# Offset convolution of a deformable convolution: 16 tiles of 32x32 reading x in place, instead of two 96x64 tiles reading shifted copies

## The chip, the cores and the metric

The kernel runs on one core of a Trainium2 chip. The metric is the device time of one execution in microseconds, median of several runs. A core has TensorE (PE, with its weight loads shown as PEld), VectorE (DVE), ScalarE (ACT), GpSimd (POOL) and SyncE (SP). Each takes its instructions in order, and they wait for one another through semaphores. Transfers are started from the queues of SP and ACT and carried out by 16 DMA engines.

## The reference

The input x has the shape (8, 16, 64, 64): batch, channels, rows, columns, in float32. Two layers follow each other. The first is layer norm, a depthwise 3x3 convolution, a channel gate, and attention in shifted 8x8 windows, which ends in a new x of the same shape. The second is a deformable convolution with batch norm, and the change is in its first step:

```python
om = conv_general_dilated(x, w_off, (1, 1), padding=[(1, 1), (1, 1)]) + b_off   # w_off: (27, 16, 3, 3)
off_y, off_x, mask = om[:, :9], om[:, 9:18], sigmoid(om[:, 18:])
py = off_y + row + ky - 1
px = off_x + column + kx - 1
# sampled = bilinear sample of x at (py, px) for each of the 9 taps, times mask
out = einsum('bckhw,ock->bohw', sampled, w) + b
return relu(batch_norm(out)) + x
```

So the offset convolution makes 27 channels for each of the 8 images: 9 vertical offsets, 9 horizontal offsets and 9 masks, from 16 input channels and 9 taps.

## The kernel before, in words

x lies on the 128 partitions as batch x channel (image b on partitions 16b to 16b+15), padded by one row and one column on each side, in the tile `xp` (66 rows of 66). PSUM is one tile `PS` of 8 banks of 512 float32 per partition.

The stages, in order: load of the constants and of x; layer norm; q, k and v; attention in a loop; a gate and the output projection, whose last step writes x into `xp` in 8 chunks of 8 rows (DVE, line 711, semaphore `xl_ready`); the **offset stage**, which this change is about; then the **sampling stage** (32 x 4 steps, lines 1297 to 1329), which takes most of the time; batch norm and the store of the result.

The offset stage goes over 8 chunks of 8 rows (512 columns of 64x8 positions). All engines follow an order that is written out by hand:

- SP copies `xp` four times three times into `xs` (line 336, 48 transfers): for each group g of two images and each kx, the 32 partitions of the group go to partitions 32kx to 32kx+31, shifted by kx columns. So the three horizontal taps stand under one another on 96 partitions. The copies go in four pieces of 16 rows, as soon as `xl_ready` says that the rows are there, and each piece has a semaphore `xs_in[j]`.
- PE, `offsets(n, u)` (line 1236): for each of two halves h, three matmuls (ky) for each of two sides accumulate 54 channels (2 images x 27) for 512 positions from 96 partitions.
- DVE (line 732) adds the bias and the column number to each of the two halves and writes them to `two[:, u]` (semaphore `om_out`). From the third chunk on it waits until the stores of the chunk two before have landed (`px_stored`).
- SP (h = 0) and ACT (h = 1) store the horizontal coordinates, 9 partitions at a time, into the scratch `px_scratch` in DRAM (`store_px`, line 315): four transfers each per chunk. ACT does this in between its evictions.
- PE, `first(n)` (line 1253): image rows for the first sampling (16 matmuls of 64x64 tiles, 144 columns, in three rounds), evicted by ACT at line 1053; and `to_samples(n, u)` (line 1260): 16 matmuls with 108 columns which transpose offsets and masks so that positions lie on partitions, evicted by ACT at lines 1061 and 1062.

PE's order is: offsets(0), offsets(1), first(0), to_samples(0), offsets(2), first(1), to_samples(1), and so on to offsets(7), first(6), to_samples(6), to_samples(7). After the last store has landed, SP loads the first coordinates back, spread over 64 partitions (`load_px`, line 345), and ACT makes the first weights of the sampling stage from them (lines 972 and 975).

At the start, SP issues x (2 of 8 chunks), the constants `cst` and the rest of x, and DVE's line 530 waits for the constants. PE's first matmuls wait for line 530. The weights of the offset convolution are laid out by DVE at lines 527 and 552.

```python
            def offsets(n, u):
                pe.wait_ge(om_out, free(n, 2))
                for h in range(2):
                    for ky in range(3):
                        for side in range(2):
                            ins = mm(PS[W * side:W * (side + 1), 2 * h + u, :], woff[0:96, ky, :],
```

Of the kernel before, what the change touches and what calls it, by code (L numbers as in the profile page):

```python
# [7 lines left out]
F32 = mybir.dt.float32  # L8
# [35 lines left out]
XS = (H + 2) * (W + 2)  # L44
# [8 lines left out]
_CCOLS = [("ident", P), ("eps_ln", 1), ("eps_bn", 1), ("bmask", B), ("bmod", PAIRS), ("h0", B), ("h1", B), ("ec", C), ("wide", 2 * P - B), ("spread", 4 * P), ("bmt", P), ("osum", P),  # L53
          ("negx", 1), ("kxadd", 1), ("xg", CH), ("pick", PAIRS * OC), ("jrel", NR),
          ("jabs", NBLK * NR), ("yabs", H * KK)]
# [15 lines left out]
def constants():  # L71
# [12 lines left out]
    put("h1", bm * (p[:, None] % C >= CS))  # L84
    put("ec", (p[:, None] % C == np.arange(C)).astype(np.float32))
# [6 lines left out]
    place = np.concatenate([[W * (g // 2) + OC * (g % 2) + k for k in range(OC)] for g in range(PAIRS)])  # L92
# [4 lines left out]
    put("xg", isx[:, None] * (np.arange(CH) % W)[None].astype(np.float32))  # L97
# [3 lines left out]
    y, k = np.meshgrid(np.arange(H), np.arange(KK), indexing="ij")  # L101
    put("yabs", (y - y % 2 + k // 3 - 1.0).reshape(1, -1) + (p // W)[:, None])
# [5 lines left out]
def build(nc, x, wpack, rpack, boff, consts, selc, out):  # L108
    ctx = ExitStack()
    with ctx:  # L110
# [6 lines left out]
        px_dram = nc.dram_tensor("px_scratch", (B, H, KK, W), F32, kind="Internal").ap()  # L117
# [7 lines left out]
        xp = sb("xp", [P, (H + 2) * (W + 2)])  # L125
        bd = sb("bd", [P, 6, P])
        MEAN, WQ, WK, WV, PO, SA = range(6)
        woff = sb("woff", [P, 3, W])
# [31 lines left out]

        xs_late = cut(PAIRS // 2 * XS)
        cut(None)
# [21 lines left out]
        xs_soon = cut2(PAIRS // 2 * XS)  # L184
        cut2(None)
# [4 lines left out]
        def xs_of(g):  # L190
            return (xs_soon, xs_late)[g // 2][:, g % 2 * XS:(g % 2 + 1) * XS]

# [67 lines left out]
        xs_in = [sem("xs_in%d" % j) for j in range(4)]  # L260
# [25 lines left out]
        def branches(eng, streams, passes):  # L286
# [6 lines left out]
            with eng.Else():  # L293
                with eng.Fori(0, PAIRS) as g:
                    with eng.Fori(0, NBLK) as band:
                        passes(g * NBLK + band, g, band)
                eng.nop()
# [25 lines left out]
        def _(sp):  # L323
# [26 lines left out]
            for u in range(2):  # L350
                sp.wait_ge(px_stored[u], 16 * B * NCH // 2)
            for line in range(0, PXR, GR):
                load_px(0, line, line)
# [1039 lines left out]
```

## Time and profile before

| | us |
|---|---|
| median of 3 runs | 880.37 (879.98 to 880.49) |
| the profiled execution, its own time | 876.57 |
| its span in the trace | 874.7 |
| busy: PE, DVE, ACT, POOL | 702.8, 723.9, 585.1, 598.7 |
| offset stage, first convolution matmul to the end of to_samples(6) | 257.09 to 325.84 |

The span is the time from the first to the last instruction in the trace. The time of an execution has a little around it (876.57 against 874.7). Engines work side by side, so their busy times don't add up to the span. What counts is who waits for whom, stage by stage.

### The profile page before, as it was taken

The numbers are of one execution on the slowest core, as the hardware profiler recorded it, in microseconds if no ns is written. First come the engines' busy times: TensorE is split into PE (matmuls) and PEld (weight loads), VectorE is DVE, ScalarE is ACT, GpSimd is POOL, SyncE is SP. The second block draws the span as 40 slices with busy tenths as digits, with TensorE's granted clock in tenths as the row PEclk, the third lists the DMA queues.
The fourth block names the chain that finished last, engine by engine and source line by source line (L and its number), as shares of the span: only waits on it lengthen the run. The fifth ranks groups of instructions, "written<-read, shape, count | busy, mean of one in ns | idle before, by whom it ended". The sixth has DMA issues, their size and how long they took to land.

```text
span 874.7 us, 30507 instructions
## 1 busy us (share of the span) xinstructions
PE 702.8 (80%) x12218; PEld 514.0 (59%) x12218; DVE 723.9 (83%) x975; ACT 585.1 (67%) x1088; POOL 598.7 (68%) x384
## 2 busy tenths in 40 slices
PE   4886888888699997888888787888888888777753
PEld 2532555656335666666667666776676666555542
DVE  1447999999532215999999999999999999999975
ACT  1445676776312327988878888879788888777615
POOL 2004887886140003989989999998899998999960
PEclk9787999999799997999999999999999999999987
DMA  4000000000076019555655555656555556555402
GB/s 165 0 1 0 1 1 0 0 0 0 0 179 150 15 22 216 158 151 141 157 164 138 152 151 143 160 138 164 156 141 146 161 143 165 159 150 152 111 3 97
DMA packets 29504, 90.77 MB, mean 104 GB/s; under 512 B 10446, under 2 KB 10574, under 8 KB 29134
## 3 DMA queue, kind: packets, MB, share of 16 engines
q1 hardware_dynamic: 26384, 88.25, 38.0%
q8 instruction: 91, 1.49, 0.8%
q10 hardware_dynamic: 3006, 0.84, 0.4%
q14 instruction: 23, 0.19, 0.1%
HBM read 79.11 MB, written 3.28 MB: 94 GB/s over the span
## 4 chain that ended last, share of the span: by engine, by line
DVE 45%; PE 33%; issue 15%; ACT 2%; DMA 2%; DVEq 1%; POOL 1%; ACTq 0%; SPq 0%; POOLq 0%
PE PS L1097 32%; DVE region L748 23%; DVE region L760 11%; DVE region L633 2%; DVE region L589 2%; DVE region L593 1%; DVE region L608 1%; DMA cst<-in_consts 1%; DVE region L595 1%; DVE region L578 1%; DVE region L590 1%; PE PS L1167 1%; DMA region<-px_scratch 1%; DVE region L575 0%; DVE region L535 0%
## 5 line engine op out<-in xcount | busy, mean ns | idle before, releaser
L1097 PE MATMUL PS<-region 64*64 64x144 f32 (+3 forms) x10112 | 459.4, 293 | 107.1 <-issue 75.7
L1097 PEld LDWEIGHTS PS<-region 64*64 64x64 f32 (+1 forms) x10112 | 343.8, 134 | 215.4 <-issue 185.5
L748 DVE TENSOR_TENSOR region<-PS,region 128x864 f32<-128x864 f32 x384 | 383.8, 1064 | 9.8 <-PE PS L1097 9.6
L488 POOL TENSOR_TENSOR region<-region 128x768 f32<-128x768 f32 x128 | 202.5, 1582 | 64.8 <-DVE region L748 64.8
L492 POOL TENSOR_TENSOR region<-region 128x864 f32<-128x864 f32 x128 | 224.1, 1751 | 18.6 <-POOL region L488 0.4
L975 ACT ACTIVATE region<-region 128x1152 f32<-128x1152 f32 x128 | 149.1, 1165 | 33.4 <-PE PS L1097 29.5
L972 ACT ACTIVATE region<-region,cst 128x1152 f32<-128x1152 f32 x128 | 159.3, 1244 | 5.7 <-DMA region<-px_scratch 4.4
L760 DVE TENSOR_REDUCE region<-region 128x32 f32<-128x960 f32 x128 | 148.3, 1159 | 1.5 <-POOL region L492 1.5
L411 POOL TENSOR_TENSOR region<-region,cst 128x1024 f32<-128x1024 f32 x32 | 61.1, 1911 | 50.5 <-ACT region L867 25.5
L1097 PE MATMUL PS<-wg,xp 64*64 64x144 f32 x1024 | 82.7, 289 | 5.4 <-issue 5.4
L1006 ACT ACTIVATE region<-x,cst (+2 forms) x288 | 86.7, 413 | 0.0
L1097 PEld LDWEIGHTS PS<-wg,xp 64*64 64x64 f32 x1024 | 67.1, 136 | 13.3 <-issue 12.2
L633 DVE SCALAR_TENSOR_TENSOR region<-region,wr (+4 forms) x57 | 73.7, 1293 | 0.1
L469 POOL TENSOR_TENSOR region<-region 128x648 f32<-128x648 f32 x32 | 41.8, 1306 | 41.5 <-ACT region L1014 41.5
L981 ACT ACTIVATE region<-PS 128x432 f32 (+3 forms) x75 | 35.9, 479 | 50.6 <-PE PS L1097 50.5
L416 POOL TENSOR_TENSOR region<-region,cst 128x512 f32<-128x512 f32 x32 | 43.9, 1373 | 1.7 <-DVE region L578 1.7
L1097 PE MATMUL PS<-region,woff 96*64 96x512 f32 x192 | 42.8, 592 | 0.8 <-DVE xp L711 0.8
L1053 ACT ACTIVATE region<-PS 128x432 f32<-128x432 f32 (+1 forms) x21 | 10.3, 490 | 45.3 <-PE PS L1097 44.8
L732 DVE SCALAR_TENSOR_TENSOR two<-PS,bcol,cst 128x512 f32<-128x512 f32 x16 | 11.3, 747 | 35.3 <-PE PS L1097 29.3
L887 ACT ACTIVATE region<-PS 128x512 f32<-128x512 f32 x32 | 19.1, 597 | 26.6 <-PE PS L1167 26.6
L882 ACT ACTIVATE region<-region 128x640 f32<-128x640 f32 x32 | 23.5, 735 | 12.4 <-DVE region L595 12.4
L1097 PEld LDWEIGHTS PS<-region,woff 96*64 96x64 f32 x192 | 16.6, 136 | 22.1 <-issue 20.5
(117 smaller groups left out, 609.9 us busy)
## 6 DMA issues: line engine op xcount, KB each, us to landing
region<-px_scratch SPq DMA_DIRECT2D x256, 288.0 KB, 4.3
out<-region SPq DMA_DIRECT2D x4, 512.0 KB, 3.0
x<-in_x SPq DMA_DIRECT2D x1, 1536.0 KB, 11.7
cst<-in_consts SPq DMA_DIRECT2D x1, 1234.5 KB, 8.6
region<-xp SPq DMA_DIRECT2D x8, 140.2 KB, 3.0
region<-xp SPq DMA_DIRECT2D x8, 140.1 KB, 3.0
region<-xp SPq DMA_DIRECT2D x8, 140.0 KB, 3.1
region<-xp SPq DMA_DIRECT2D x8, 132.0 KB, 2.5
```

The lines of the kernel that those rows point to most:

```text
L411: pool.tensor_tensor(kb[:, u].rearrange("p w (b k) -> p w b k", b=B), kw[:, bass.ds(n * 2 * K1, 2 * K1)].rearrange("p (w k) -> p w k", w=2 ...
L416: pool.tensor_tensor(kvb[:, u].rearrange("p w t (b k) -> p (w t) b k", b=B), kv[:, bass.ds(n * 4 * K2, 4 * K2)].rearrange("p (w k) -> p w ...
L469: pool.tensor_tensor(aw4[:, rows], aw4[:, rows], mk4[:, rows, bass.ds(g, 1), :].rearrange("p r g k -> p (r g) k").unsqueeze(3).to_broadcas ...
L488: pool.tensor_tensor(two_rows[:, :, :, 0:2 * THIRD - KEEP], two_rows[:, :, :, 0:2 * THIRD - KEEP], two_rows[:, :, :, KEEP:2 * THIRD], ALU. ...
L492: pool.tensor_tensor(two_rows[:, :, :, 0:THIRD], two_rows[:, :, :, 0:THIRD], two_rows[:, :, :, 2 * THIRD:NA], ALU.add).then_inc(fold_ready, 1)
L633: ins = v.scalar_tensor_tensor(dst, src, wcol, dst, ALU.mult, ALU.add)
L748: v.tensor_tensor(uu[:, 2 * u:2 * u + 2, :, THIRD * t:THIRD * (t + 1)], PS[:, 2 * t:2 * t + 2, 0:THIRD * C].rearrange("p h (a o) -> p h o ...
L760: v.tensor_reduce(totals(2 * (n % STEPS), n // STEPS), uu[:, b:b + 2, :, 0:KEEP], AX.X, ALU.add).then_inc(os_ready, 1)
L972: a.activation(rows, rows, ACT.Abs, bias=c_("negx")).then_inc(ab_ready, 1)
L975: a.activation(wt[:, i % 2].rearrange("p q k s -> p (q k s)"), rows, ACT.Relu, bias=1.0, scale=-1.0).then_inc(wt_ready, 1)
L1006: a.activation(aw4[:, rows, :, j], py4[:, rows, bass.ds(g, 1), :].rearrange("p r g k -> p (r g) k"), ACT.Abs, bias=c_("jrel")[:, NR - 1 - ...
L1097: return nc.tensor.matmul(o, l, r, start=start, stop=stop)
```

## The change

1. The copies `xs` go, with their 48 transfers and semaphores. PE reads `xp` itself. The 128 partitions are four row groups r of 32 (two images each). A matmul takes one tap t (of 9), one row group r, one of two row pairs d of each group of four rows, and one of two images e of the group. It writes 27 channels to the partitions 32(2d+e) and up, bank r, for 256 positions. The weights of the other image are zero (`e01`). So a chunk has 9 x 4 x 2 x 2 = 144 matmuls of a 32x32 tile each, 288 pairs of weight load and matmul.
2. All four banks 0 to 3 belong to one chunk, so `offsets(n)` now waits for `om_out` of chunk n-1, not of n-2.
3. DVE's two evictions have the same size, each from two half banks. `two` now has another order of positions, and the picks of `to_samples` follow it: as many matmuls, with 2x54 columns.
4. `store_px` makes two transfers per chunk on each of SP and ACT, of 9 x 16 x 64, instead of four of 9 x 8 x 64, into a scratch ordered by chunk, row pair, image, group. `load_px` reads pieces of the same size, 1152 contiguous values, spread over 64 partitions.
5. The constants shrink from 2469 to 1712 columns (`xg` is halved, and `yabs`, which only the branch for large offsets uses, is split in two). `woff` grows from 192 to 576 columns, `xp` by two rows, and `b_off` is loaded in four transfers instead of two.

```diff
-_CCOLS = [... ("xg", CH), ("pick", PAIRS * OC), ("jrel", NR),
-          ("jabs", NBLK * NR), ("yabs", H * KK)]
+_CCOLS = [... ("e01", 2), ... ("xg", CH // 2), ("pick", PAIRS * OC), ("jrel", NR),
+          ("jabs", NBLK * NR), ("yrow", H), ("kadd", KK)]
...
-        def store_px(eng, n, u, h):
-            for g in range(PAIRS):
-                row = W * (g // 2) + OC * (g % 2) + KK
-                eng.dma_start(px_dram[g + h * PAIRS, bass.ds(n * RPC, RPC)].rearrange("r k c -> k r c"),
-                              two[row:row + KK, u, h * CH:(h + 1) * CH].rearrange("p (r c) -> p r c", c=W)).then_inc(px_stored[u], 16)
+        def store_px(eng, n, u, d):
+            for e in range(2):
+                row = 32 * (2 * d + e) + KK
+                eng.dma_start(px_dram[n, d, e].rearrange("r i q k c -> k (r i q) c"),
+                              grid(two[row:row + KK, u, :], W)).then_inc(px_stored[u], 16)
...
-            edges = [0] + [16 * j + 1 for j in range(1, 4)] + [H + 2]
-            for j in range(4):
-                sp.wait_ge(xl_ready, done(2 * j + 1))
-                for g in range(PAIRS):
-                    for kx in range(3):
-                        a, b = (W + 2) * edges[j], (W + 2) * edges[j + 1] - kx
-                        sp.dma_start(xs_of(g)[32 * kx:32 * (kx + 1), a:b], xp[32 * g:32 * (g + 1), a + kx:b + kx]).then_inc(xs_in[j], 16)
...
                 for h in range(2):
-                    v.scalar_tensor_tensor(two[:, n % 2, h * CH:(h + 1) * CH], PS[:, 2 * h + n % 2, :],
-                                           bcol[:, :], c_("xg"), ALU.add, ALU.add).then_inc(om_out, 1)
+                    v.scalar_tensor_tensor(grid(two[:, n % 2, h * CH:(h + 1) * CH], CH // 2), PS[:, 2 * h:2 * h + 2, 0:CH // 2],
+                                           bcol[:, :], mid(c_("xg"), 2), ALU.add, ALU.add).then_inc(om_out, 1)
...
-            def offsets(n, u):
-                pe.wait_ge(om_out, free(n, 2))
-                for h in range(2):
-                    for ky in range(3):
-                        for side in range(2):
-                            ins = mm(PS[W * side:W * (side + 1), 2 * h + u, :], woff[0:96, ky, :],
-                                     grid(xs_of(2 * h + side), W + 2)[0:96, n * RPC + ky:n * RPC + ky + RPC, 0:W], start=ky == 0, stop=ky == 2)
-                    ins.then_inc(om_ready, 1)
+            def offsets(n):
+                pe.wait_ge(om_out, done(n - 1, 2))
+                for t in range(KK):
+                    for r in range(4):
+                        part = slice(32 * r, 32 * (r + 1))
+                        for d in range(2):
+                            y = n * RPC + 2 * d + t // 3
+                            src = xp4[part, y:y + RPC, t % 3:t % 3 + W].rearrange("p (i b q) c -> p i b q c", i=2, b=2)[:, :, 0]
+                            for e in range(2):
+                                j = 2 * d + e
+                                ins = mm(PS[32 * j:32 * (j + 1), r, 0:CH // 2], woff[part, e, t, :], src, start=t == 0, stop=t == KK - 1)
+                ins.then_inc(om_ready, 2)
...
-                if n in (0, 1, 3, 5):
-                    pe.wait_ge(xs_in[(n + 1) // 2], 16 * 3 * PAIRS)
-                offsets(n, n % 2)
+                offsets(n)
```

PE's order in the offset stage, before (`region` is the tile that holds `xs`):

```order
L1097 MATMUL PS<-two,bd 128x512 x24
L1097 MATMUL PS<-region,woff 64x512 x24
L1097 MATMUL PS<-wg,xp 64x144 x16
L1097 MATMUL PS<-cst,two 64x108 x16
L1097 MATMUL PS<-region,woff 64x512 x12
L1097 MATMUL PS<-wg,xp 64x144 x16
```

and of the change:

```order
L1085 MATMUL PS<-two,bd 128x512 x24
L1085 MATMUL PS<-xp,woff 32x256 x288
L1085 MATMUL PS<-wg,xp 64x144 x16
L1085 MATMUL PS<-cst,two 64x2x54 x16
L1085 MATMUL PS<-xp,woff 32x256 x144
L1085 MATMUL PS<-wg,xp 64x144 x16
```

The place of each step stays; only the convolution has 144 matmuls of 256 columns in the place of 12 of 512.

SP's queue before, from the start of the program to the first loads of coordinates:

```order
L325 DMA x<-in_x 128x1024
L326 DMA cst<-in_consts 128x2469
L327 DMA x<-in_x 128x3072
L336 DMA region<-xp 32x1122
L336 DMA region<-xp 32x1121
```

```order
L336 DMA region<-xp 32x1120
L319 DMA px_scratch<-two 9x8x64 x32
L345 DMA region<-px_scratch 64x1152 x8
```

and of the change:

```order
L322 DMA x<-in_x 128x1024
L323 DMA cst<-in_consts 128x1712
L324 DMA x<-in_x 128x3072
L316 DMA px_scratch<-two 9x16x64 x16
L334 DMA region<-px_scratch 64x1152 x8
```

The 48 copies are gone from SP's queue, the constants are shorter, and there are 16 stores instead of 32, each twice as large.

## Rows read from the trace of the kernel before

**Rows 1.** The page: the span, and the chain that ended last, by engine and line.
```profile
span 874.7 us, 30507 instructions
...
DVE 45%; PE 33%; issue 15%; ACT 2%; DMA 2%; DVEq 1%; POOL 1%; ACTq 0%; SPq 0%; POOLq 0%
```
**Rows 2.** The chain in order of time, offset stage: start us, us, what.
```profile
257.09 68.75 PE PS L1097 x640
325.84 0.02 issue
325.86 0.29 ACT x L1061
...
326.94 1.59 DMA px_scratch<-two
```
**Rows 3.** PE's timeline, first convolutions and one chunk: start us, us, engine, line, operation, tiles.
```profile
257.09 10.52 PE L1097 MATMUL PS<-region,woff 96*64 96x512 f32 x48 [0.84 <-DVE xp L711]
...
271.29 5.37 PE L1097 MATMUL PS<-region,woff 96*64 96x512 f32 x24
276.59 2.29 PE L1097 MATMUL PS<-wg,xp 64*64 64x144 f32 x32
278.81 1.75 PE L1097 MATMUL PS<-cst,two 128*64 128x108 f32 x32
280.34 5.37 PE L1097 MATMUL PS<-region,woff 96*64 96x512 f32 x24
```
**Rows 4.** PEld's timeline, convolution before: two loads per round.
```profile
257.57 0.14 PEld L1097 LDWEIGHTS PS<-region,woff 96*64 96x64 f32 x2 [0.29 <-issue]
258.00 0.14 PEld L1097 LDWEIGHTS PS<-region,woff 96*64 96x64 f32 x2 [0.29 <-issue]
```
**Rows 5.** Windows in the sampling stage, four 64x64 tiles: instructions in each in brackets.
```profile
core 0: us, PE busy (x) PEld busy (x) DVE busy (x) ACT busy (x) POOL busy (x), PEclk, DMA share, GB/s
360.38:360.40 0.02, 0.00 (x1) 0.02 (x1) 0.02 (x1) 0.02 (x1) 0.02 (x1) 1.00 0.58 231
360.40:360.42 0.02, 0.02 (x4) 0.02 (x4) 0.02 (x1) 0.02 (x1) 0.02 (x1) 1.00 0.00 0
...
489.07:492.07 3.01, 3.01 (x96) 3.00 (x96) 3.01 (x5) 0.83 (x2) 3.01 (x3) 1.00 0.39 101
```
**Rows 6.** DVE's timeline, evictions of the offset stage (line 732).
```profile
267.66 1.41 DVE L732 SCALAR_TENSOR_TENSOR two<-PS,bcol,cst 128x512 f32<-128x512 f32 x2 [3.74 <-PE PS L1097]
```
**Rows 7.** Who waited for whom, 257 to 326 us.
```profile
DVE two L732 <- PE PS L1097: 29.3, 7, 5.5
...
DVE two L732 <- DMA px_scratch<-two: 6.1, 1, 6.1
```
**Rows 8.** PE's granted clock (PEclk) in windows: before the stage, one chunk, its end.
```profile
253.00:257.00 4.00, 2.57 (x6) 0.67 (x4) 1.47 (x2) 0.53 (x1) 1.26 (x1) 1.00 0.92 213
...
280.00:289.00 9.00, 9.00 (x93) 5.46 (x89) 2.02 (x4) 2.31 (x7) 0.00 (x0) 1.00 0.13 24
...
326.00:336.40 10.40, 3.80 (x46) 2.92 (x47) 1.49 (x5) 4.08 (x11) 0.00 (x0) 0.78 0.65 155
```
**Rows 9.** PE's timeline at the end of the stage: waits in square brackets.
```profile
326.85 1.72 PE L1097 MATMUL PS<-cst,two 128*64 128x108 f32 x32 [1.02 <-ACT region L1062]
...
336.43 1.00 PE L1097 MATMUL PS<-region 64*64 64x144 f32 x12 [2.57 <-ACT region L975]
```
**Rows 10.** The start: transfers (size, us to landing), the chain, and a window.
```profile
x<-in_x SPq DMA_DIRECT2D x1, 1536.0 KB, 11.7
cst<-in_consts SPq DMA_DIRECT2D x1, 1234.5 KB, 8.6
x<-in_x SPq DMA_DIRECT2D x1, 512.0 KB, 4.9
...
1.20 8.56 DMA cst<-in_consts
9.79 0.24 DVE bd L530
...
6.00:8.00 2.00, 0.00 (x0) 0.00 (x0) 0.00 (x0) 0.00 (x0) 0.00 (x0) 1.00 0.86 284
```
**Rows 11.** DVE's timeline before the reciprocal: weights of the convolution laid out.
```profile
28.59 1.01 DVE L552 TENSOR_TENSOR woff<-wr,cst 32x162 f32<-32x162 f32 x3
30.39 1.75 DVE L560 RECIPROCAL two<-two 128x256 f32<-128x256 f32 x1 [0.42 <-ACT two L858]
```
**Rows 12.** ACT's queue at the end of the offset stage: four stores.
```profile
325.88 0.28 ACTq L319 DMA_DIRECT2D px_scratch<-two  x1
326.19 0.34 ACTq L319 DMA_DIRECT2D px_scratch<-two  x1
326.57 0.73 ACTq L319 DMA_DIRECT2D px_scratch<-two  x2
```

More of the change, by code:

```diff
@@ L91, in constants @@
     put("negx", -(p[:, None] % W).astype(np.float32))
-    place = np.concatenate([[W * (g // 2) + OC * (g % 2) + k for k in range(OC)] for g in range(PAIRS)])
+    place = np.concatenate([32 * j + np.arange(OC) for j in range(4)])
     ch = np.full(P, -1)
@@ L293, in branches @@
             with eng.Else():
-                with eng.Fori(0, PAIRS) as g:
-                    with eng.Fori(0, NBLK) as band:
-                        passes(g * NBLK + band, g, band)
+                if pairs_written_out:
+                    for g in range(PAIRS):
+                        with eng.Fori(0, NBLK) as band:
+                            passes(g * NBLK + band, g, band)
+                else:
+                    with eng.Fori(0, PAIRS) as g:
+                        with eng.Fori(0, NBLK) as band:
+                            passes(g * NBLK + band, g, band)
                 eng.nop()
@@ L360, in load_ahead @@
                         sp.wait_ge(wt_ready, done(s * SPC + line // GR))
-                        load_px(g, c * RPC + line, line)
+                        load_px(g, c, line)
             def pass_px(p, g, band):
@@ L367, in pass_px @@
                 for line in range(0, PXR, GR):
-                    load_px(g, line, line)
+                    load_px(g, 0, line)
                 with sp.Fori(0, NCH - 1) as c:
@@ L526, in _ @@
             v.memset(bcol[:, :], 0.0).then_inc(woff_zero, 1)
[L527 removed]
+            v.memset(woff[:, :, :, :], 0.0).then_inc(woff_zero, 1)
             dve.wait_ge(w_in, 48)
@@ L549, in _ @@
             dve.wait_ge(woff_zero, 2)
[L550 to L556 removed]
+            for e in range(2):
+                v.tensor_scalar(woff[:, e, :, 0:OC], w_("woff").rearrange("p (t k) -> p t k", k=OC), c_("e01")[:, e:e + 1], None, ALU.mult).then_inc(bd_ready, 1)
+            dve.wait_ge(b_in, 64)
             v.tensor_scalar(bcol[:, :], bcol[:, :], c_("kxadd"), None, ALU.add).then_inc(bd_ready, 1)
@@ L833, in _ @@
             act.wait_ge(woff_zero, 2)
-            for half in range(2):
-                act.dma_start(bcol[W * half:W * half + 2 * OC, :], boff[2 * OC * half:2 * OC * (half + 1), :]).then_inc(b_in, 16)
+            for j in range(4):
+                act.dma_start(bcol[32 * j:32 * j + OC, :], boff[OC * j:OC * (j + 1), :]).then_inc(b_in, 16)
             for s, n in ((k_out, 2), (q_staged, 4), (ln_ready, 2), (sq_ready, 2), (q_out, 2), (v_out, 2), (exp_ready, 2), (vt_out, 6), (pt_out, 4),
@@ L1263, in to_samples @@
                 pe.wait_ge(mk_out, done(n - 1, 2))
-                for r in range(RPC):
-                    for h in range(2):
-                        q, line = r % 2, 2 * (r // 2) + h
-                        ins = mm(PS[64 * q:64 * (q + 1), 4 + line // 4, (line % 4) * PAIRS * OC:(line % 4 + 1) * PAIRS * OC],
-                                 two[:, u, h * CH + r * W:h * CH + (r + 1) * W], c_("pick"))
+                for r in range(4):
+                    for i in range(2):
+                        for q in range(2):
+                            at = r // 2 * PAIRS * OC + r % 2 * 2 * OC
+                            ins = mm(PS[64 * q:64 * (q + 1), 4 + i, 0:4 * PAIRS * OC].rearrange("p (d a) -> p d a", d=2)[:, :, at:at + 2 * OC],
+                                     two[:, u, r * CH // 2 + (2 * i + q) * W:r * CH // 2 + (2 * i + q + 1) * W],
+                                     grid(c_("pick"), 2 * OC))
                 ins.then_inc(tr_ready, 1)
```

62 lines of the change are left out of this document (26 added, 36 removed).

## The prediction

> **What bounds the kernel now.** I began with the page. The chain that ended last is 45% DVE and 33% PE [rows 1]. Over the whole span that says little, since most of it is the sampling stage, where DVE's products and PE's taps alternate. The change doesn't touch that stage: the same instructions with the same shapes. So the question is only what bounds the offset stage and the start.
>
> The chain in order of time answers it. From 257.09 us to 325.84 us it is PE alone, with no wait in between [rows 2]. So each microsecond that PE gains or loses there moves everything behind it, and what other engines or transfers do there is hidden as long as PE never waits for them. PE's timeline shows the chunks: the convolution starts at 271.29, the image rows at 276.59, the transposes at 278.81, the next convolution at 280.34 [rows 3]. That is 5.30 + 2.22 + 1.53 = 9.05 us per chunk, of which the convolution is 5.30.
>
> How are these 5.30 us made up? Weight loads come in twos, 0.43 us apart [rows 4]: two tiles side by side (partitions 0 to 63 and 64 to 127 of PSUM) work at once, and each instruction of 512 columns holds its tile for 0.43 us. 24 instructions on 2 tiles are 12 rounds, 12 x 0.43 = 5.16 us, and some 0.14 us is the changeover to the next kind of tile.
>
> **Part 1: the convolution on 16 tiles.** A chunk now has 288 instructions of 256 columns. If an instruction holds its tile in proportion to its columns, that is 0.215 us, and if all 16 tiles work at once there are 288 / 16 = 18 rounds: 18 x 0.215 = 3.87 us. Add the same changeover, 0.14 us, and the stagger of the tiles' starts. For that the sampling stage has the nearest row: where it starts on four 64x64 tiles, the counts of matmuls and of weight loads under way both go from 1 to 4 between 360.38 and 360.42 us [rows 5]. So a tile is set going within 0.005 to 0.01 us of the one before, and 16 tiles within about 0.1 us. Together 4.1 us in the place of 5.30, **1.2 us less per chunk, 9.6 us over 8 chunks**.
>
> No row shows 16 tiles at work, so I bound this from both sides. The best case is the one just worked out. For the other end: the densest long stretch has 96 pairs in 3.01 us, 0.031 us each [rows 5]. Its four tiles with 144 columns would give 0.43 x 144 / 512 / 4 = 0.030 us by themselves, so what held it was the tiles, and the row says only that a pair can be issued in 0.031 us, or faster. At that price a chunk would take 288 x 0.031 = 8.9 us, and 0.14. I take the best case because the burst in rows 5 shows pairs starting at least three times as fast as 0.031, and 16 tiles need 0.215 / 16 = 0.0134 us per pair, which is slower than the burst.
>
> [...]
>
> **Part 2: one set of banks.** `offsets(n)` now waits until DVE has taken chunk n-1 out of PSUM. Two evictions take 1.41 us [rows 6]. For n from 2 on, image rows and transposes of the chunk before (2.22 + 1.53 = 3.75 us) lie in between, so they cover the eviction and its 0.2 us of signals. If the cover were gone it would cost 1.6 us per chunk. But offsets(1) follows offsets(0) directly. There PE stands for 1.41 us plus about 0.1 us on each side, and the last matmuls must drain: **+1.7 us, once**. Could an eviction be late? It waits for the stores of the chunk two before. Before, one such wait of 6.1 us fell on DVE [rows 7], with SP's queue behind the copies. With the copies gone, SP's two stores start as soon as the chunk is evicted, and ACT's two after its evictions of the chunk before, over one period (7.8 us) before they are wanted. So it doesn't cost anything. Queued behind DVE's eviction is only its `peak` step, for which nobody waits before the end.
>
> PE's clock is 1.00 in the stage [rows 8]. At its end, where PE waits 1.0 to 2.6 us at a time [rows 9], it is 0.78 over 10.4 us [rows 8]. The new wait of 1.7 us could lower it for the second convolution. Upper bound: 4.1 us more if all of that ran at half clock. I take 0, since from 253 to 257 us PE stood for 1.4 of 4 us and the clock stayed at 1.00 [rows 8].
>
> **Part 3: the copies.** 48 transfers go from SP's queue. PE never waited for them: the first convolution started right behind DVE's last row of x, [rows 3], and the chain holds no copy [rows 2]. What hid them was PE's own work. **0 us.** The image rows and transposes keep their number and columns: 0 us. DVE's evictions have the same 512 values per partition, 0 us.
>
> **Part 4: the start.** DVE's line 530 waits for the constants, landed 8.56 us after their issue, and the chain runs through them [rows 10]. They shrink from 2469 to 1712 columns, by 1234.5 x 757 / 2469 = 378 KB. At the 284 GB/s of the stretch 6 to 8 us [rows 10] that is 1.35 us. [...] The two larger setups on DVE have a cover: `woff` is cleared while DVE waits for the constants, and the new pair of operations at line 552's place (about as long as the three of 1.01 us) ends before ACT's result, 0.42 us of idle time later [rows 11]. All later steps up to the convolution hang on this chain, and the first half of x has landed at about 6 us, the rest only 1.3 us behind the constants and not needed before. **-1.0 us.**
>
> **Part 5: the end of the stage.** The chain goes through ACT's store of the last chunk, 1.59 us [rows 2]. ACT's queue issues four transfers from 325.88 to 327.3 us [rows 12]; with two it is done some 0.4 us earlier, but each has twice the pieces. Bounds 0 and -0.7, I take **-0.2 us**. The loads of coordinates have the same size, 0 us.
>
> **The sum.** -9.6 + 1.7 - 1.0 - 0.2 = **-9.1 us**. The profiled execution took 876.57 us, so it would take 867.5. The median of the runs is 880.37, 3.8 us above the profiled one. I carry the difference over to the median: 880.37 - 9.1 = **871.3 us**.
>
> **The rivals.**
>
> *A: PE's issue is the bound.* The stage asks PE for a pair each 0.0134 us over 3.9 us, more than twice the pace of any long stretch here (0.031 [rows 5]). If the pace of that stretch were a limit of issue, the convolution would take 8.9 + 0.14 = 9.1 us, 3.8 us more per chunk, 30 us in all; with +1.7 and -1.2 that is 880.4 + 31 = **911 us**. It decides the sign where a pair costs more than (5.30 - 0.14) / 288 = 0.018 us. For it: no row shows a long stream that is faster. Against: the burst of rows 5, and that the tiles alone explain 0.030 us.
> [...]
>
> *B: column tiles of one row group don't all stream at once.* Four column tiles read four streams of x from the same 32 partitions; the trace shows at most two streams from the same partitions (two column tiles of the 64x64 tiles [rows 5]). If only two run at a time, a chunk needs 36 rounds, 36 x 0.215 + 0.24 = 8.0 us, +2.7 x 8 = +21.4, and +0.5: **902 us**.
>
> *C: in part.* The tiles overlap, but the round is longer than 0.215 us (a fixed part for each instruction, in-order starts that leave a tile waiting, a slower clock after the new wait). With 0.24 us per round a chunk takes 18 x 0.24 + 0.24 = 4.56 us, and the sum is -0.74 x 8 + 0.5 = -5.4 us; with 0.28 it is nothing: **875 to 881 us**.
>
> *D: no change.* The convolution just breaks even at 0.28 us a round: within 1.8 us of 880.4.
>
> **How the numbers follow.** A measurement of this kernel tells about 0.2%, 1.8 us, from no change. The forecast (16 tiles at full pace) gets 0.62, with 868 to 874 us from the bounds of parts 4 and 5 and some clock loss. C on the fast side of 0.2% gets 0.15. D gets 0.06. A gets 0.10 and B 0.04, and mixed cases slower by a little 0.03. So faster 0.77, same 0.06, slower 0.17. The range goes from 867.5 to 885: it leaves out A and B, 0.14, and a little below.
>
> **What would show it.** In the profile after: the convolution's groups on PE start about 4.1 us ahead of the image rows, and a chunk's period is 7.8 us instead of 9.05. Weight loads of 32 columns are under way by the dozen. One wait of PE for DVE's line 717, 1.6 us, between the first two convolutions and none later. DVE's wait for the stores is gone. The constants land at about 8.7 us instead of 9.76. The prediction is wrong if the convolution takes over 5.3 us per chunk (A or B: A if the starts are evenly spaced at one distance whatever the tile, B if the rounds come in halves), or if PE waits at each chunk.

## The result and the profile after

| | before | after |
|---|---|---|
| median | 880.17 us (875.60 to 880.49, 4 runs) | 894.48 us (889.96 to 898.04, 4 runs) |
| profiled execution, its own time | 876.57 | 893.57 |
| its span | 874.7 | 891.8 |
| offset stage, first convolution matmul to the end of to_samples(6) | 257.09 to 325.84, 68.75 us | 257.38 to 342.35, 84.97 us |

The change makes the kernel slower by 1.7% (ratio 1.0172, 95% interval 1.0114 to 1.023). The prediction was 871.3 us, with a range up to 885.0. Sign and range were both wrong.

Where did the 17.1 us of the span come from? The stage took 16.2 of them, and began 0.3 later. From its end to the first sampling matmul it is 10.6 us in both (325.84 to 336.43, 342.35 to 352.98), and the rest of the difference is 0.5. So only the stage is to be explained. The page, and the chain in order of time, of the kernel after:

```profile
span 891.8 us, 34648 instructions
...
q8 instruction: 107, 1.75, 0.9%
...
DVE 46%; PE 32%; issue 16%; ACT 2%; DMA 2%; DVEq 1%; POOL 1%; ACTq 0%; SPq 0%; POOLq 0%
```
```profile
265.26 4.29 PE PS L1085 x179
269.55 0.55 issue
```

Before, the chain had PE alone for 68.75 us [rows 2]. Now there are pieces of "issue" between its matmuls: time in which PE waited for nothing that the profile shows. PE's timeline, with the columns of [rows 3], shows them. They don't lie at one place of a chunk. From one to the next it is always a multiple of 128 pairs of weight load and matmul, all kinds counted:

```profile
257.38 4.76 PE L1085 MATMUL PS<-xp,woff 32*32 32x256 f32 x236 [0.85 <-DVE xp L696]
262.36 1.39 PE L1085 MATMUL PS<-xp,woff 32*32 32x256 f32 x52 [0.23 <-issue]
265.26 4.29 PE L1085 MATMUL PS<-xp,woff 32*32 32x256 f32 x204 [1.50 <-DVE two L717]
270.10 2.03 PE L1085 MATMUL PS<-xp,woff 32*32 32x256 f32 x84 [0.55 <-issue]
...
275.91 5.19 PE L1085 MATMUL PS<-xp,woff 32*32 32x256 f32 x235
281.80 1.40 PE L1085 MATMUL PS<-xp,woff 32*32 32x256 f32 x53 [0.70 <-issue]
283.13 2.29 PE L1085 MATMUL PS<-wg,xp 64*64 64x144 f32 x32
285.35 1.70 PE L1085 MATMUL PS<-cst,two 128*64 128x108 f32 x32
286.98 5.52 PE L1085 MATMUL PS<-xp,woff 32*32 32x256 f32 x267
...
311.53 2.77 PE L1085 MATMUL PS<-xp,woff 32*32 32x256 f32 x128 [0.36 <-issue]
315.26 2.04 PE L1085 MATMUL PS<-xp,woff 32*32 32x256 f32 x86 [0.96 <-issue]
```

A chunk begins at 275.91 and the next at 286.98: 11.07 us, of which the convolution is 7.22, where 7.8 and 4.1 were predicted (before 9.05 and 5.30, [rows 3]). Two things are in these 7.22 us. PE stands for 0.70 us with its next matmul not there. And in the stretches without a gap it is slow too: the first 236 pairs in 4.76 us are 0.020 us each, where 16 tiles at work all the time would need 0.0134, by the prediction's own estimate (0.215 / 16). (The 235 in 5.19 us hide a wait: the weight loads stood for 0.33 us at 278.35, while matmuls were still under way.)

The waits of the stage, by engine and releaser, with sum, count and longest:

```profile
DVE two L717 <- PE PS L1085: 49.4, 8, 7.0
...
PE PS L1085 <- issue: 5.9, 10, 1.0
PE PS L1085 <- DVE two L717: 1.5, 1, 1.5
```

Only one of PE's waits is for an engine that the change concerns, and DVE's wait for the stores (6.1 us in [rows 7]) is gone. The last view is of the DMA queues, with packets, MB and share. In the windows 257 to 325 us of before and 257 to 342 us of after, the queue of instructions has:

```profile
q8 instruction: 5, 0.08, 0.5%
```
```profile
q8 instruction: 21, 0.34, 1.7%
```

So 21 packets of the instruction queue came in by DMA while the stage ran, and 0.34 MB in 21 packets are 16 KB each: a packet is called a block from here on. A chunk of after has 288 pairs of the convolution and 64 of image rows and transposes, 704 instructions with the weight loads. The stage has eight convolutions and seven of the rest, 5504 instructions. Over 21 blocks that is 262 of PE's instructions per block. The two gaps that lie 128 pairs apart (311.53 and 315.26) say 256, by estimate of 64 bytes each (16 KB / 256). Between these two it is 3.73 us for one block; over the stage one block came each 4.0 us (85 / 21), against one in 13.6 us before.

### The profile page after: what moved, and what is told of

The parts are those of the page before. It is cut to its first block, busy times and chain, and to the rows that moved or that the text cites. A ratio compares the mean times of both kernels' runs of the same rounds, so it can differ in the third digit from the quotient of the medians.

```text
span 891.8 us, 34648 instructions
## 1 busy us (share of the span) xinstructions
PE 710.4 (80%) x14330; PEld 528.1 (59%) x14330; DVE 723.8 (81%) x974; ACT 585.4 (66%) x1088; POOL 598.6 (67%) x384
## 4 chain that ended last, share of the span: by engine, by line
DVE 46%; PE 32%; issue 16%; ACT 2%; DMA 2%; DVEq 1%; POOL 1%; ACTq 0%; SPq 0%; POOLq 0%
PE PS L1085 31%; DVE region L733 23%; DVE region L745 11%; DVE region L618 2%; DVE region L574 2%; DVE region L578 1%; DVE region L593 1%; DMA cst<-in_consts 1%; DVE region L580 1%; DVE region L563 1%; PE PS L1155 1%; DVE region L575 1%; DMA region<-px_scratch 0%; DVE region L560 0%; DVE region L524 0%
## 5 line engine op out<-in xcount | busy, mean ns | idle before, releaser
L745 DVE TENSOR_REDUCE region<-region 128x32 f32<-128x960 f32 x128 | 145.7, 1138 | 1.5 <-POOL region L481 1.5
L1085 PE MATMUL PS<-xp,woff 32*32 32x256 f32 x2304 | 50.6, 385 | 8.0 <-issue 5.7
L1041 ACT ACTIVATE region<-PS 128x432 f32<-128x432 f32 (+1 forms) x21 | 10.3, 491 | 61.8 <-PE PS L1085 61.3
L1085 PEld LDWEIGHTS PS<-xp,woff 32*32 32x32 f32 x2304 | 33.8, 103 | 23.1 <-issue 10.1
```

What stands on the lines that cost most here:

```text
L745: v.tensor_reduce(totals(2 * (n % STEPS), n // STEPS), uu[:, b:b + 2, :, 0:KEEP], AX.X, ALU.add).then_inc(os_ready, 1)
L1085: return nc.tensor.matmul(o, l, r, start=start, stop=stop)
```

## The experiments

Two causes are called F and W from here on. **F** stood at the start: the supply of instructions bounds PE. If the measured 3.73 us for a block between two gaps and 4.0 us over the stage are the best that it gives, 704 instructions (2.75 blocks) cost 10.2 to 11 us whatever they do. **W** came up after the first loops had run. Its measured part: with 16 tiles in turn a tap takes 0.65 us in the loop, where the prediction took 0.43. The rest of W is my conjecture, which no trace here shows: PE starts pairs in order and holds only so many that wait for a busy tile, so that behind the second pair of a float32 matmul, which goes to the same tile as the first, other tiles would stand empty. The time that a pair keeps its tile is called its hold: by estimate 0.215 us for 256 columns, half of the 0.43 us that [rows 4] show for 512, and in the same proportion for other lengths. The other theories are named in the expectations. What stays comparable between kernels is the stage; what lies behind it varied from 547 to 556 us between profiles, whatever the stage did. Each diff is against the changed kernel. Kernels with one profiled run are given by that run, beside the median of before on the same chip.

### Half the columns

```
-  src = ...[:, :, 0]                            mm(PS[..., r, 0:CH // 2], ...)
+  src = ...[:, 0:2 if n == 0 else 1, 0]         mm(PS[..., r, 0:CH // (2 if n == 0 else 4)], ...)
```

> The change, but from chunk 1 on each convolution matmul covers 128 of its 256 columns (the other half of the positions keeps chunk 0's values). As many instructions, half the array work. Theory F (PE's instructions come from memory in blocks of 256, one block each 3.9 us at best, and that is the bound): the period per chunk stays at 10.9 to 11.1 us as in the change, the whole time within 3 us of the change. Rival H (a tap costs three rounds of the tiles' own hold time, no fetch bound): the convolution takes 9 x 0.325 + 0.25 = 3.2 us, the period is 6.9 us, 29 us less than the change. Rival S (pairs are supplied at 20 ns each, whatever their columns, no fetch bound): period 9.85 us, 9 us less.

Measured: 895.93 us (before 878.65). With half of PE's work in the convolution taken away the kernel is no faster. PE's timeline:

```profile
277.75 3.56 PE L1085 MATMUL PS<-xp,woff 32*32 32x128 f32 x235
283.15 0.97 PE L1085 MATMUL PS<-xp,woff 32*32 32x128 f32 x53 [1.84 <-issue]
284.05 2.29 PE L1085 MATMUL PS<-wg,xp 64*64 64x144 f32 x32
...
322.48 3.58 PE L1085 MATMUL PS<-xp,woff 32*32 32x128 f32 x233
...
257.00:344.00 87.00, 71.65 (x2746) 59.10 (x2746) 14.75 (x23) 18.16 (x55) 3.00 (x3) 0.88 0.09 17
```

The 235 matmuls before the gap take 3.56 us instead of 5.19, and the gap grows from 0.70 to 1.84. From 277.75 to 322.48 it is 44.73 us for four chunks, where the full kernel takes 45.18 for the same four (275.91 to 321.09). Part of that is the clock: the last row is the window of the stage, and the granted clock is 0.88 on average. Three of the four chunks had it at 0.84 to 0.86, and their image rows took 3.0 to 4.0 us instead of 2.29. The two chunks at 1.00 throughout (from 277.75 and from 322.48) took 10.15 and 9.91 us, where the same chunks of the full kernel took 11.07 and 10.23. So at an equal clock half of the columns gives back 0.9 and 0.3 us a chunk, where a period set by the tiles would have fallen to 6.9. A fixed 0.020 us from start to start would give 9.85, close to these two, but the 235 pairs are 0.015 us apart and the rest is gaps. The gaps took the place of the work (1.84 us for 0.70 behind the 235th matmul), and F holds as the main bound.

### A loop in place of nine taps in a row

Taps 0 and 1 are in a loop of four rounds, then comes tap 8, and each matmul overwrites instead of adding up. The count and shape of the matmuls are the same, but only 3/9 of the convolution's instructions stand in the program.
```
-  for t in range(KK): ...
+  with pe.Fori(0, 4) as again:
+      tap(0)
+      tap(1)
+  ins = tap(8)
```

> The change, but the nine taps are a loop of four passes over taps 0 and 1 and then tap 8: as many executed instructions and as much array work, yet only 96 of 288 pairs per chunk lie in the program (the taps in between are left out and each tap overwrites, so the offsets hold tap 8 alone). Theory F: about 332 instructions have to be fetched per chunk, 5.1 us, no longer a bound, the gaps marked issue go, and the period falls to 9.85 us (if a tap keeps its 0.65 us) or 7.9 us (if it falls to 0.43), 9 to 22 us less in all than the change. If fetch is no bound, the period stays at 11.07 us.

Measured: 888.9 us (before 878.65), the stage 256.08 to 332.80, 76.7 us. PE's gaps are gone (first fence, its timeline), and fewer blocks are fetched (second, the queue from 262 to 318 us: 7 here, 14 in the run before in the same window, 4.0 us each):

```profile
273.76 5.91 PE L1085 MATMUL PS<-xp,woff 32*32 32x256 f32 x288
279.60 2.29 PE L1085 MATMUL PS<-wg,xp 64*64 64x144 f32 x32
...
283.45 5.91 PE L1085 MATMUL PS<-xp,woff 32*32 32x256 f32 x288
```
```profile
q8 instruction: 7, 0.11, 0.9%
```
```profile
q8 instruction: 14, 0.23, 1.7%
```

With the supply out of the way the period is 9.69 us, 1.4 less than after, but still above the 9.05 of before: a convolution takes 5.84, 0.65 us per tap. So F alone is not the whole; even with this supply of instructions the change would lose. A little of the 5.84 is the loop's own: the weight loads stand for 0.22 us at each turn, here in the chunk that begins at 283.45.

```profile
284.69 1.04 PEld L1085 LDWEIGHTS PS<-xp,woff 32*32 32x32 f32 x64 [0.22 <-issue]
285.95 1.04 PEld L1085 LDWEIGHTS PS<-xp,woff 32*32 32x32 f32 x64 [0.22 <-issue]
```

A turn of two taps is 1.26 us from load to load. In the kernel after, 267 loads in a row took 5.04 us, 1.21 for two taps.

### The loop, with half and with a quarter of the columns

The first has the edits of the two runs before together; the second 64 columns instead of 128.

> The loop of e2_loop with 128 of 256 columns from chunk 1 on (left out: the same taps, and half of the positions). Fetch is no bound here by theory F, so this shows what sets the 0.65 us per tap of the change. H (three rounds of hold time per tap): the convolution takes 3.2 us and the period 6.95. S (20 ns per pair whatever the columns): the convolution stays at 6.1 us, the period at 9.85.

Measured: 882.99 us (before 878.65), period 8.37 us (275.29 to 283.65), convolution 4.51.

```profile
275.29 4.58 PE L1085 MATMUL PS<-xp,woff 32*32 32x128 f32 x288
...
283.65 4.58 PE L1085 MATMUL PS<-xp,woff 32*32 32x128 f32 x288
```

This speaks for F as well: as many matmuls of the same shape as in the first experiment, 8.37 instead of 10.15 and 9.91 us, all three at a clock of 1.00, when they come from a loop. For the tap it fitted neither value on record: 4.51 us lies between them.

> The loop of e2_loop with 64 of 256 columns from chunk 1 on (left out: the taps in between and three quarters of the positions). 256 columns gave 0.65 us per tap, 128 gave 0.50. Theory P with a floor: at 64 columns the tap stays near 0.50 us and the convolution near 4.5 us, since 32 pairs at 0.0156 us are the pace of the supply. Without a floor the two points give a straight line, 0.35 + 1.38 x the hold time of 0.054: 0.42 us per tap, convolution 3.8 us.

Measured: 883.54 us (before 878.53), convolution 3.88 us.

```profile
283.29 3.94 PE L1085 MATMUL PS<-xp,woff 32*32 32x64 f32 x288
287.16 2.29 PE L1085 MATMUL PS<-wg,xp 64*64 64x144 f32 x32
```

A tap takes 0.65, 0.50 and 0.43 us with holds of 0.215, 0.108 and 0.054 us by estimate. There is no floor at 0.50, and 288 pairs in 3.88 us are 0.0135 us each, with the turns of the loop in them; the 64 loads of one turn take 0.69 us, 0.011 each. So PE did start pairs at the pace that the prediction asked of it, 0.0134 us, with this shortest hold. At 128 columns the turns of the loop show in the tap: without a loop 139 loads of 128 columns took 1.87 us (first experiment, from 287.90), 0.43 us per tap and not 0.50.

### Two taps in a row on each tile

In the loop, taps 0 and 1 are taken on one tile before the next, so four pairs in a row go to the same tile. Work and number of instructions are those of the loop.
```
-  for e in range(2):
-      j = 2 * d + e
-      mm(PS[32 * j:32 * (j + 1), ...], woff[part, e, t, :], src)
+  for e in range(2):
+      j = 2 * d + e
+      for t in ts: ...
```

> The loop of e2_loop (9.69 us period, 5.84 of it convolution, 0.65 per tap), with the order of the matmuls changed so that each tile gets taps 0 and 1 in a row, four pairs instead of two (left out: the taps in between, as in e2_loop). Theory P (pairs reach the array at one pace, about 0.020 us): the convolution stays at 5.8 us. Rival W (PE takes its instructions in order and can hold only so many that wait for a busy tile): four pairs in a row for one tile block the others for longer, the convolution takes 7 us or more.

Measured: 921.63 us (before 878.53), 8.96 us per convolution where the loop had 5.84. That is 25 us of the 32.7 more than the loop's 888.9. Some 9 us are the clock: behind the wait of 1.57 us it was 0.54 from 271.40 to 293.39, and the second convolution took 16.25 us. From there on it was 1.00.

```profile
293.39 9.03 PE L1085 MATMUL PS<-xp,woff 32*32 32x256 f32 x288
302.35 2.29 PE L1085 MATMUL PS<-wg,xp 64*64 64x144 f32 x32
```

Nothing but the order has changed, so no fixed pace of pairs sets the tap. What the run shows is that the order alone costs 3.12 us per convolution. That fits W, but how many pairs PE holds, or whether later ones pass waiting ones, no trace shows.

### Half of the tiles

One run leaves out the second image of each pair from the second chunk on (`for e in range(2 if n == 0 else 1)`), the other two of the four groups of rows (`for r in range(4 if n == 0 else 2)`). Both have eight tiles of 32x32 in turn.

> The change's kernel, but from the second chunk on only the first image of each pair is convolved (the other keeps the first chunk's sums): eight tiles of 32x32, in all four groups of rows, two groups of columns each. A chunk has 144 + 64 pairs, 416 instructions, so the supply of instructions is no limit. If the number of tiles in turn is what costs PE its 0.22 us per tap (W): 4.1 us of convolution per chunk, as eight tiles of 32x64 took. If the small tile itself is slow: more, up to 5.8. Time of the kernel by W: stage about 85 - 7x(11.07 - 7.93) = 63 us, 872.

> As the run before, but what is left out from the second chunk on is the rows r = 2 and 3: eight tiles of 32x32 in two groups of rows, four groups of columns each, so that four tiles read streams from the same 32 partitions, as in the full change. By W (the number of tiles in turn) 4.1 us of convolution per chunk as well, time 872. If four streams from one group of rows are the cause of the 0.22 us (rival B of the prediction in a weak form): 0.65 us per tap, 5.8 us per chunk, time about 884.

Measured: 872.43 and 879.16 us (before 878.59). Once the clock is at full speed, the convolution is the same in both, 4.05 us, 0.45 per tap: two holds of 0.215 and 0.02. First fence: four groups of rows, two of columns. Second: two groups of rows, four of columns.

```profile
274.79 4.12 PE L1085 MATMUL PS<-xp,woff 32*32 32x256 f32 x144
278.84 2.29 PE L1085 MATMUL PS<-wg,xp 64*64 64x144 f32 x32
```
```profile
267.44 7.07 PE L1085 MATMUL PS<-xp,woff 32*32 32x256 f32 x144 [1.50 <-DVE two L717]
274.43 4.10 PE L1085 MATMUL PS<-wg,xp 64*64 64x144 f32 x32
...
280.17 4.12 PE L1085 MATMUL PS<-xp,woff 32*32 32x256 f32 x144
284.22 2.29 PE L1085 MATMUL PS<-wg,xp 64*64 64x144 f32 x32
...
267.40:278.50 11.10, 11.06 (x178) 7.70 (x178) 1.41 (x2) 1.06 (x2) 0.00 (x0) 0.55 0.11 21
```

So neither the small tile nor four streams from the same 32 partitions cost anything beyond that 0.02 us per tap, and rival B is out. What costs is that 16 tiles are in turn (0.65 us per tap in the loop against 0.45). The 6.7 us between the two runs are mostly a thing of their own, seen in the second fence, whose last row is a window with the columns of [rows 5]. Behind the wait of 1.50 us the granted clock was 0.55 over 11 us, and the second chunk took 4.8 us longer (12.73 instead of 7.91). This is common: of the ten profiles with this wait, the clock behind it stayed at 1.00 over the second chunk in four (after, the loop, eight tiles of 32x64, the first of these two), and was 0.54 to 0.85 in six. The upper bound that part 2 named, 4.1 us, does occur, then, and with two taps in a row on each tile it was 9 us.

### Eight tiles of 32x64, all of the work

The weights of both images of a pair stand side by side in a tile of 64 columns. A chunk has 72 matmuls, 144 pairs, each still of 256 columns.
```
-  woff = sb("woff", [P, 2, KK, 2 * C])
+  woff = sb("woff", [P, KK, W])
...
-  for e in range(2):
-      j = 2 * d + e
-      ins = mm(PS[32 * j:32 * (j + 1), r, 0:CH // 2], woff[part, e, t, :], src, ...)
+  ins = mm(PS[W * d:W * (d + 1), r, 0:CH // 2], woff[part, t, :], src, ...)
```

> The change with eight tiles of 32x64 instead of sixteen of 32x32: the weights of both images of a row group stand side by side (54 columns), so a chunk has 72 matmuls, 144 pairs, with the same 18 rounds of 256 columns. Theory F: 424 instructions per chunk to fetch, 6.5 us, below PE's own 7.85 us, so no gaps marked issue, convolution 4.1 us, period 7.85, and the time is 9 us below the kernel before (868 to 874 where that takes 880). With S beside it the same, since 16 pairs per tap at 20 ns are 0.33 us, below 0.43. With H the tap still takes three rounds, convolution 6.1 us, period 9.85, time about 886.

Measured: 871.43 us (867.81 to 876.19, 12 runs) against 878.65 (17 runs), **ratio 0.9916, interval 0.9892 to 0.994: faster than both kernels**. Stage 258.61 to 319.93, 61.3 us.

```profile
272.27 4.15 PE L1086 MATMUL PS<-xp,woff 32*64 32x256 f32 x144
276.34 2.29 PE L1086 MATMUL PS<-wg,xp 64*64 64x144 f32 x32
278.57 1.70 PE L1086 MATMUL PS<-cst,two 128*64 128x108 f32 x32
280.20 4.15 PE L1086 MATMUL PS<-xp,woff 32*64 32x256 f32 x144
```

Convolution 4.07, period 7.93: what the prediction had said of the 16 tiles. Per chunk there are 416 instructions, 1.6 blocks, by estimate 6.5 us at the measured 4.0 each, less than PE's 7.93.

The control for it cuts each of these matmuls into two of 128 columns: the same tiles and the same columns, twice the instructions (704 per chunk again).
```
+  for i in range(2):
+      ins = mm(PS[W * d:W * (d + 1), r, CH // 4 * i:CH // 4 * (i + 1)], woff[part, t, :], src[:, i], ...)
```

> The kernel of e4_eight_tiles with each convolution matmul split in two of 128 columns: the same tiles and the same array work, but 288 pairs per chunk as in the change. Theory F (one block of 256 instructions per 3.9 us): the period goes from 7.93 us back to 10.9 to 11.1, the stage is 24 us longer than in e4_eight_tiles, about 893 to 897 us in all, although the tiles are wide and few. If instead sixteen narrow tiles are what is slow, the convolution stays at 4.1 us and the time at 871 to 875.

Measured: 899.39 us (before 878.53), some 2 us above what F said. The stage is 84.7 us (256.30 to 341.04), 23.4 longer than with whole matmuls, about the 24 that F said; the rest lies behind it.

```profile
275.33 4.82 PE L1086 MATMUL PS<-xp,woff 32*64 32x128 f32 x235
281.02 1.43 PE L1086 MATMUL PS<-xp,woff 32*64 32x128 f32 x53 [0.87 <-issue]
...
286.23 5.52 PE L1086 MATMUL PS<-xp,woff 32*64 32x128 f32 x267
```

The period is 10.9 us again, with the gap behind the same 235th matmul as in the kernel after: the period hangs on the number of instructions, not on the tiles.

### Two chunks at once

The chunks lie side by side in a bank, so a matmul has 512 columns and there are half as many of them: `offsets(m)` for two chunks, `to_samples(n)` after each. This on eight tiles:

> Eight tiles of 32x64, and one convolution for two chunks: 512 columns per matmul, banks 0 to 3 used whole, then image rows and transposes of both chunks. Half of e4's convolution pairs, and the wait of 1.57 us between the first two convolutions goes. Theory F: no gaps marked issue; the convolution of two chunks takes 18 x 0.43 + 0.25 = 8.0 us; the stage takes about 59.7 us against e4's 61.3, the time is 1 to 2 us below e4 and 10 us below the kernel before (about 869 where that takes 879).

Measured: 875.61 us against 878.53, ratio 0.9966 (0.9948 to 0.9983). The 869 us expected were missed: the stage took 66.5 us and not 59.7. The convolution was as expected (7.93 for two chunks), but PE had a new wait in the image rows, five times:

```profile
264.91 1.69 PE L1086 MATMUL PS<-wg,xp 64*64 64x144 f32 x24
267.90 0.71 PE L1086 MATMUL PS<-wg,xp 64*64 64x144 f32 x8 [1.30 <-ACT region L1042]
```

ACT evicts them, and stood in its order behind the wait for DVE's second half and the stores. The next kernel puts these two behind the image rows:

> Eight tiles, 512 columns for two chunks, as the run before; ACT now evicts the image rows of a chunk before it waits for the second half's coordinates and issues their stores. If that order made PE wait (five waits of 1.3 to 1.9 us in the run before), they go: the stage takes 4x7.93 us of convolution, 7x2.22 of image rows and 7x1.63 of the small constant rows and some waits, about 60 us from its first matmul to the end, and the kernel 868 to 870 us where before takes 878.5. If ACT is late for another reason (too much work of its own for two chunks at a time), the waits stay and the time is 875 as in the run before.

Measured: 871.20 us (6 runs) against 877.70, ratio 0.9933 (0.991 to 0.9956). Four of the five waits are gone, and one of 1.94 us is left. The expected 868 to 870 was missed by over a microsecond, and it does no better than eight tiles with one chunk. Then the same on 16 tiles:

> Sixteen 32x32 tiles as in the change, but 512 columns for two chunks at once: half as many instructions per column. F (instruction supply): 576 + 256 + some 12 instructions per two chunks are 3.3 blocks, at 3.9 us each 12.9 us, less than PE needs, so no waits on issue; the 22 blocks of the stage become about 14. W (a limited number of pairs waits for busy tiles, a tap takes 0.35 + 1.38 x hold with a hold of 0.43): 0.94 us per tap, 8.5 to 8.7 us of convolution per two chunks, time 871 to 873. If a tap takes three holds whatever the hold (0.65 for 0.216): 1.29 us per tap, 11.7 us of convolution per two chunks, time about 884. If sixteen tiles work at their full rate with long holds: 0.86 us per tap, 7.9 us, time 868 to 870 as the eight tiles.

Measured: 880.11 us (12 runs) against 877.70, ratio 1.001 (0.9989 to 1.003).

```profile
275.39 9.76 PE L1085 MATMUL PS<-xp,woff 32*32 32x512 f32 x288
285.08 2.29 PE L1085 MATMUL PS<-wg,xp 64*64 64x144 f32 x32
```

No gap on issue: F's half came out. The time was no better than before, where W's line had said 871 to 873. The tap takes 9.69 / 9 = 1.08 us, where W's line from the short holds said 0.94 and three holds would be 1.29. So that line is wrong. Taken over all four lengths, a tap on 16 tiles costs two holds and 0.32, 0.28, 0.22, 0.22 us (at 64, 128, 256 and 512 columns), the first three in loops whose turns are in the number; without one it is 0.21 at 128 columns (0.43 us, above). On eight tiles it costs two holds and 0.02.

## Why the prediction was wrong

**The step that failed is part 1, "if all 16 tiles work at once"**: 18 rounds x 0.215, with 0.0134 us per pair. Its test was the burst in [rows 5], four pairs within 0.02 us. It shows the start of four pairs and nothing of a long stream. There the runs found two things that it left out: instructions arrived at one block per 4.0 us, and 16 tiles in turn took 0.65 us per tap in the loop and not 0.43. Against the predicted stage of 60.9 us (68.75 - 9.6 + 1.7), after is 24.1 us longer, and the runs divide that:

- Supply of instructions (F): after 84.97, with the loop 76.72, so 8.3 us. In the stage's steady part it is 1.4 us per chunk.
- 16 tiles in turn (W): the loop's 76.72 against the 61.32 of eight tiles, 15.4 us. (5.84 - 4.07) x 8 = 14.2 of it is the tap; the other 1.2 us lie in three convolutions of the loop that took 6.35, 6.51 and 5.98 us at a clock of 1.00, for a reason not found. The turns of the loop are in these 15.4 us too, at most 0.22 us each.
- Eight tiles against the sum: 0.4 us. The sum was right for a kernel with half as many instructions.

The two don't add up freely: half the columns took PE's work away and the period fell by 0.3 to 0.9 us at most, since the supply alone costs 10 to 11 us (9.91 and 10.15 measured there at a clock of 1.00).

The 0.031 us of [rows 5] was rightly read as the tiles' limit. The slow end, 8.9 us per chunk, was too far, and the measured 7.07 on average over the stage (84.97 less 7 x 3.85 of rows and transposes and the wait of 1.5, over 8) lies between the ends. I put 0.62 on the fast end because a burst spoke for it. Rows that show nothing of a long stream deserved more for the middle.

**Rival A** had the right kind (what brings instructions to the array, not the array) and the right sign; it had 0.10, and its price of 911 us was 17 too high. The point from which it decides, 0.018 us per pair, was right: measured are 7.07 / 288 = 0.0245. The pace of 0.031 us is no limit of issue, though: the quarter-column loop starts pairs 0.0135 us apart over 3.88 us. The 0.0245 comes from the two causes above. **Rival B** is ruled out by the two runs with half of the tiles. **Rival C** named "in-order starts that leave a tile waiting" as one of its causes; that is W's conjecture, and at the measured 0.65 us per tap the convolution takes 5.84 us, which is already more than 5.30.

**Part 2** (+1.7, once): 1.50 us of wait, and 1.51 from the end of the first convolution (263.75) to the second (265.26). DVE's evictions ran from 263.80 to 265.21, so there were 0.05 us on each side where 0.1 had been taken. Right. The clock stayed at 1.00 here, as taken, but that was luck: in six of the ten profiles with this wait it did not, and the clock deserved a term of its own. **Part 3** (0): right, no wait for stores is left, but the image rows and transposes take 3.85 instead of 3.75 us. **Part 4** (-1.0): the constants landed earlier, but what came of it did not show. The chain after, and one piece of it before:

```profile
1.20 7.91 DMA cst<-in_consts
...
14.55 3.72 PE PS L1085 x6
```
```profile
15.19 2.00 PE PS L1097 x6
```

7.91 us instead of 8.56 [rows 10], 0.65 less, where 1.35 had been worked out and 1.0 taken. No run shows what the step from 1.35 to 1.0 rests on: from 0 to 14 us SP's queue moved 2.97 MB at 59.7% of the 16 DMA engines after, 3.36 MB at 66.7% before, which is 22.2 and 22.5 GB/s per busy engine. Then six matmuls took 3.72 us that had taken 2.00 before, which cost more than was gained. Their first four took 2.08 us instead of 1.13, and did so in two more profiles (half the columns, eight tiles of 32x64), but not in those of the first two loops, whose program is the same there: it changes with the execution and is not the change's. The first convolution then began 0.3 us later. Over the profiles of the experiments it began between 256.1 and 260.9, so a gain of this size can't be told there. **Part 5** (-0.2): from the end of the stage to the first sampling matmul 10.63 instead of 10.59 us, so nothing.

**What stays open.** A packet of the instruction queue takes 1.1 us by its share (1.7% of 16 engines x 85 us, over 21), while blocks come 4.0 us apart. What passes in the rest was not tried. How many pairs PE can hold waiting isn't measured either, nor that it has such a limit: eight tiles in turn lose next to nothing, 16 lose 0.22 us per tap, and no run lies between. That the loss comes from waiting pairs is argued and not shown, from two things: the order alone makes it worse (8.96 us for 5.84), and half the tiles remove it (0.45 us per tap). A third fact doesn't fit well: if tiles stand empty behind waiting pairs, the loss should grow with the hold, and it was 0.21 us at 128 columns and 0.22 at 512. What is shown is that 16 tiles in turn cost it, not by what.

## What to carry to other kernels

Smaller tiles multiplied the instructions here (704 per chunk against 176 before), so before you count rounds, count instructions per microsecond, weight loads included, over a stretch of more than one block. This kernel got 256 in 3.7 to 4 us and no more, and the signs were 21 packets on the instruction queue in 85 us and "issue" gaps at multiples of 128 pairs. Here fewer instructions did the same work faster: eight tiles of 32x64 took 4.07 us per convolution with 288 instructions, where 16 tiles of 32x32 took 7.22 with 576. The burst of four pairs in 0.02 us proved nothing for 288 pairs, which took 0.0245 us each; the control that tells is to change the number of instructions with the work held (a loop, or a split), and the work with their number held.

## What was not expected of the hardware

- TensorE ran short of instructions: one block of 16 KB per 4.0 us over a stage (21 in 85 us; 14 in 56 us in two more kernels), 3.73 us between two gaps one block apart, from the first convolution on (0.23 us of gap behind the first 236 matmuls). It cost 8.3 us of a stage of 84.97.
- With the taps in a loop PE had none of these gaps, and the stage was shorter by 8.3 us (76.72 for 84.97). Each turn stopped the weight loads for 0.22 us, which 256 columns mostly covered (two taps in 1.26 us from load to load, 1.21 without a loop); with 64 columns a turn's 64 loads took 0.69 us and the stop came on top. (One gap on PE, of 0.22 us, came with 64 columns.)
- With 16 tiles in turn, a tap of two pairs per tile costs two holds and 0.21 to 0.22 us (0.43, 0.65 and 1.08 us at 128, 256 and 512 columns); with eight tiles, of 32x32 or of 32x64, two holds and 0.02 (0.45 us at 256 columns). The hold itself is an estimate, 0.43 us per 512 columns.
- Four tiles that read from the same 32 partitions took no longer than two that do: 4.05 us for 144 pairs on eight tiles in both runs.
- The wait of 1.5 us left the clock at 1.00 in four of ten profiles. In the six others it was 0.54 to 0.85 over the chunk behind the wait; in one of them, 0.55 for 11 us, the chunk was 4.8 us longer.
